# A decoder layer's feed-forward reordered: logits ahead of the shared chunks, an exclusive scan, tiles turned one product sooner

## The chip, the cores and the metric

The kernel runs on one core of a Trainium2 chip. Its time is the device time of one execution in microseconds; the kernel before has a median of 443.64 us in three runs (443.29 to 444.85).

## The reference

A decoder layer for 32 sequences of 128 tokens with 128 features: self attention, attention to a context of 77 tokens, and a feed-forward part with 16 experts, each behind a layer norm and added to x. The change lies in the feed-forward part alone:

```python
logits = hidden @ router_w.T                       # 4096 x 16
top_vals, top_idx = jax.lax.top_k(logits, 1)
scores = sigmoid(top_vals)                         # one expert of 16 per token
gate_up = einsum('nth,nhf->ntf', hidden * scores, gate_up_proj)
routed_out = einsum('ntf,nfh->nth', up * silu(gate), down_proj)
shared = (silu(hidden @ shared_gate_w.T) * (hidden @ shared_up_w.T)) @ shared_down_w.T   # 512 wide
x = x + shared + expert_sum
```

The kernel computes a token's expert only where it is chosen: it sorts the 4096 normalised rows by expert into tiles of 128 rows, each expert's part padded to whole tiles, 47 tiles in all, runs each tile through its expert's weights and scatters the results back.

## The kernel before

**Work.** Tokens are taken in 8 groups of 4 sequences (512 columns). The shared feed-forward of a group is 4 chunks of 128 hidden units, 32 chunks in all. A chunk is: gate product (L1360) and up product (L1361) on TensorE, silu of the gate on ScalarE into `s_g`, product of both on VectorE into `act[c]` (`gated`, L1115), and the down products (L1351) that add up over 4 chunks in one bank, which VectorE adds to `xs` (`add_down`, L1120). A tile n is: load of its rows (`t_row`, issued by ScalarE, L1310) and of its expert's 192 KB of weights (`t_w`, issued by SP, L1444), turn on TensorE (L1397), copy to `t_hT` on ScalarE (L1288), gate and up products (L1406, L1407), silu (L1292), product on VectorE (L1198), down product (L1425), copies of row numbers and result on VectorE (L1204, L1205), and an indirect scatter to `routed` by POOL (L1337).

**Order.** Every engine runs its own written list in order; semaphores join them, no planner is involved. At the end of the attention TensorE turns the normalised rows of a group (`turn_h`), ScalarE copies them to `xT` (`copy_h`), and TensorE makes their logits in bank 1 (`logits`, L1084). With each of the 8 groups one half of a chunk of group 0 goes along (`half_chunk`: even ones gate, odd ones up), so four chunks' gate and up products are made by then. VectorE takes `gated` of chunks 0 to 2, and then, once all logits are there, the maximum (L1129), the one-hot of the first maximum (L1131 to L1135), and the gating score. TensorE counts tokens per expert and ranks them with two products on the one-hot (L1370, L1372), an inclusive scan adds the counts up (L1146), a subtraction makes it exclusive (L1147), six operations on 16 columns make each expert's first tile, three wide ones and a reduction make each token's slot `pos` (L1164). Then `owner`, each tile's expert, follows (L1167 to L1170), on which SP waits. `gated` and `add_down` of groups 0 and 1 stand between these steps. ScalarE scales the normalised rows by their score, four at a time with each of the first 8 chunks from chunk 4 on (L1265); POOL scatters 128 rows at a time, 32 times, to `sorted_in` (L1332).

**Ahead, among and behind the tiles.** The chunks of 6 groups (24) come ahead of the tiles. Of the other 8, three stand among the tiles (behind tiles 14, 28, 42: gate and up in one piece in TensorE's list, down two tiles later), one ahead of the last tile's down product, four behind the tiles. Tile loops are written a tile or two ahead: in turn n, TensorE makes the gate and up products of tile n+1, turns tile n+2 into the single bank 0, and makes tile n's down product; ScalarE copies tile n+2, applies silu to n+1 and issues the row load of tile n+6; VectorE multiplies n+1 and moves n out. There are rings of 8 buffers for rows, weights and results, `t_hT`, `t_sg` and `t_act` have two. ScalarE issues the first 8 row loads once all 32 scatters have landed. SP reads 8 owners into registers, issues 8 weight loads, reads the next 8, and so on; from tile 8 on a load waits for the down product eight tiles back. In the end SP waits for all scatters, loads `routed` back in four pieces, VectorE adds them to `xs` and SP stores 8 groups.

Of the kernel before, what the change touches and what calls it, by code (L numbers as in the profile page):

```python
# [29 lines left out]
def decoder_layer(nc, t, out):  # L30
# [26 lines left out]
    with ExitStack() as ctx:  # L57
# [891 lines left out]
        def act_phase3(a):  # L949
# [38 lines left out]
            deviation3(a, 1)  # L988
# [40 lines left out]
        cum = sb4("cum", [P, N_LG])  # L1029
# [74 lines left out]
        def dve_phase4(v):  # L1104
# [18 lines left out]
            for c in range(CH - 1):  # L1123
                gated(0, c)
# [4 lines left out]
            v.tensor_reduce(best[:], lg3, AX.X, ALU.max).then_inc(s["lg"], 1)  # L1129
            v.wait_ge(s["lg"], 1)  # L1130
# [9 lines left out]
            gated(0, 3)  # L1140
# [4 lines left out]
            cum3 = cum[:].rearrange("p (n b) -> p n b", b=B)  # L1145
            step(v.tensor_tensor_scan(out=cum[:], data0=onesf[:], data1=bank[BK_COUNT][:], initial=0.0, op0=ALU.mult, op1=ALU.add))  # L1146
            step(v.tensor_tensor(tot[:], cum[:], bank[BK_COUNT][:], ALU.subtract))  # L1147
            gated(1, 0)
            first, last = tot3[:, :, 0], cum3[:, :, B - 1]
# [29 lines left out]
            add_down(AHEAD_OF_TILES - 1, (AHEAD_OF_TILES - 1) % 2)  # L1179
# [5 lines left out]
            def behind_add(g):  # L1185
                v.wait_ge(s["downp"], g + 1)
                x_g = seqs(xs, g).rearrange("p j f -> p (j f)")
                v.tensor_tensor(x_g, bank[BEHIND_DOWN[g - AHEAD_OF_TILES]][:], x_g, ALU.add).then_inc(s["x3"], 1)

            def add_routed(g):  # L1190
                if g % 2 == 0:
                    v.wait_ge(y_in[g // 2], 16)
                v.wait_ge(s["x3"], max(g + 1, AHEAD_OF_TILES))
                v.tensor_tensor(xs[:, g * JP:(g + 1) * JP], xs[:, g * JP:(g + 1) * JP], seqs(y_back[g // 2], g % 2), ALU.add).then_inc(s["res_add"], 1)
# [12 lines left out]
            def body(n, r, k):  # L1207
                if not last_tile(n, 1):
                    mul(n + 1, (r + 1) % RING)
                leave(n, r, k)  # L1210
                if n - 1 in MIXED:
                    behind_gated(MIXED[n - 1])
            mul(0, 0)
            loop_tiles(body)
            behind_gated(3)
            behind_gated(4)
            behind_add(6)
            behind_gated(5)
            add_routed(0)
            add_routed(1)  # L1220
            behind_gated(6)
            add_routed(2)
            add_routed(3)
            behind_gated(7)
# [14 lines left out]
        BEHIND_DOWN = (5, 4)  # L1239
        TILE_TURN, TILE_DOWN = 0, (1, 4)  # L1240

        def behind_banks(m):
            return (2, 3) if m in (4, 6) else (6, 7)
# [12 lines left out]
        def act_phase4(a):  # L1256
# [40 lines left out]
            def body(n, r, k):  # L1297
                if not last_tile(n, 2):
                    turned(n + 2, (r + 2) % RING)
                if not last_tile(n, 1):  # L1300
                    gated(n + 1, (r + 1) % RING)
                if n in MIXED:
                    behind_silu(MIXED[n])
                if n >= 2 and not last_tile(n, RING - 2):
                    load_rows(n + (RING - 2), (r + RING - 2) % RING)

            def load_rows(n, r):
                if n >= RING:
                    a.wait_ge(s["ty"], n - (RING - 1))
                a.dma_start(t_row[r][:], sorted_in[bass.ds(n * P, P)]).then_inc(t_in[r], 16)  # L1310
            a.wait_ge(s["scat"], B * 16)
            for r in range(RING):
                load_rows(r, r)
# [4 lines left out]
            for m in range(len(MIXED), BEHIND):  # L1318
                behind_silu(m)

        def pool_phase4(p):
            p.wait_ge(s["bp"], 4 * (NG - 2) * JP)
            p.memset(onesf[:], 1.0)
            p.memset(h_rows[:, :, D:ROW], 0.0).then_inc(s["h_kept"], 1)
# [16 lines left out]
        def pe_phase4(pe):  # L1341
            for g in range(2, NG):
# [3 lines left out]
                half_chunk(pe, g)  # L1346
# [9 lines left out]
            def shared(g, par):  # L1356
                for c in range(CH):
# [9 lines left out]
                    if g == 0 and c == 2:  # L1367

# [3 lines left out]
                        pe.matmul(bank[BK_RANK][:], before[:], oh_b[:], start=True, stop=True).then_inc(s["rankp"], 1)  # L1372
            loop_shared(pe, shared)
            down(AHEAD_OF_TILES - 1, (AHEAD_OF_TILES - 1) % 2, CH - 1)

            def behind_gate_up(m):
                pe.wait_ge(s["act"], BASE + (m if m <= len(MIXED) else m - 1))
                gate, up = behind_banks(m)
                g, c = AHEAD_OF_TILES + m // CH, m % CH
                pe.matmul(bank[gate][:], sg[:, c * P:(c + 1) * P], xT[:, g * GT:(g + 1) * GT], start=True, stop=True)  # L1380
                pe.matmul(bank[up][:], su[:, c * P:(c + 1) * P], xT[:, g * GT:(g + 1) * GT],
                          start=True, stop=True).then_inc(s["gup"], 1)

            def behind_down(m):
                c = m % CH
                pe.wait_ge(s["act"], BASE + m + 1)
                for j in range(JP):
                    i = pe.matmul(bank[BEHIND_DOWN[m // CH]][:, j * D:(j + 1) * D], act[c][:, j * P:(j + 1) * P], sd[:, c],
# [4 lines left out]
            def turn(n, r, k):  # L1393
                pe.wait_ge(t_in[r], k * 32 + 32)
                if n >= 1:
                    pe.wait_ge(s["tT"], n)
                i = pe.transpose(bank[TILE_TURN][:, 0:P], t_row[r][:, 0:D], ident[:])  # L1397
                i.then_inc(s["tTp"], 1)

            def gate_up(n, r):  # L1400
                pe.wait_ge(s["tT"], n + 1)
                if n >= 2:
                    pe.wait_ge(s["tact"], n - 1)
                if n == 1:
                    pe.wait_ge(s["x3"], AHEAD_OF_TILES - 1)
# [3 lines left out]
            def body(n, r, k):  # L1409
                if not last_tile(n, 1):  # L1410
                    gate_up(n + 1, (r + 1) % RING)
                if not last_tile(n, 2):
                    turn(n + 2, (r + 2) % RING, (n + 2) // RING)
                if n in MIXED:
                    behind_gate_up(MIXED[n])
                if n - 2 in MIXED:
                    behind_down(MIXED[n - 2])
                if last_tile(n, 1):
                    behind_gate_up(len(MIXED))
                pe.wait_ge(s["tact"], n + 1)  # L1420
                if n >= 2:
                    pe.wait_ge(s["ty"], n - 1)
                if n == 1:
                    pe.wait_ge(s["x3"], AHEAD_OF_TILES)
# [6 lines left out]
            pe.wait_ge(s["ty"], TILES)  # L1431
            for m in range(len(MIXED) + 1, BEHIND):
                behind_gate_up(m)
# [3 lines left out]
        def sp_phase4(sp):  # L1437
# [8 lines left out]
            load_ring(0, False)  # L1446
            for k in range(1, -(-TILES // RING)):
# [119 lines left out]
```

## Time and profile before

| | |
|---|---|
| median of 3 runs | 443.64 us |
| profiled execution | 446.38 us, span 444.5 us |
| TensorE products, weight loads | 380.0 us (85%), 291.8 us (66%) |
| VectorE, ScalarE, POOL | 282.3 us (63%), 255.3 us (57%), 195.9 us (44%) |
| mean granted TensorE clock | 0.97 |
| moved | 61.83 MB, mean 139 GB/s |

The page cuts the span into 40 slices of 11.1 us and gives in tenths how busy each engine was; the feed-forward part begins at about slice 26. A digit of the DMA row is the mean over the core's 16 transfer engines.

```profile
PE   2789877886768999899899998899999978898894
...
ACT  3688898887446677776777775435532223333311
POOL 1397677555013546555620000000577717676730
PEclk9999999999868999999999999879999999999998
DMA  8962235675827656566610000000061137788629
```

A busy engine need not be the bound: a share is a mean over stages, and what a stage costs is read from the waits in it.

### The profile page before, as it was taken

What the parts mean: (1) busy time and instruction counts of PE and PEld (TensorE: products, weight loads), DVE (VectorE), ACT (ScalarE), POOL (GpSimd) and SP (SyncE); (2) the same over time, 40 slices, a digit from 0 to 9 for tenths busy, and PEclk for the clock granted to TensorE, in tenths of its full rate; (3) what the DMA queues carried; (4) which work ended last, traced back from release to release, by engine and by line L of the source; (5) the groups of instructions that cost most, each with busy time, mean ns of one, the idle gap of its engine ahead of it and who ended that gap; (6) DMA issues with size and microseconds to landing.
All of it is one profiled execution on the core that took longest, in us unless ns stands there. A gap on an engine that the chain in (4) does not pass through costs nothing.

```text
span 444.5 us, 10412 instructions
## 1 busy us (share of the span) xinstructions
PE 380.0 (85%) x3691; PEld 291.8 (66%) x3691; DVE 282.3 (63%) x837; ACT 255.3 (57%) x611; POOL 195.9 (44%) x280
## 2 busy tenths in 40 slices
PE   2789877886768999899899998899999978898894
PEld 1466655664546888888888887675566656677663
DVE  4566999989477777877877736527633324444436
ACT  3688898887446677776777775435532223333311
POOL 1397677555013546555620000000577717676730
PEclk9999999999868999999999999879999999999998
DMA  8962235675827656566610000000061137788629
GB/s 268 350 192 67 97 97 149 182 189 160 253 73 216 155 165 186 159 177 191 193 45 6 5 4 2 1 1 0 32 196 56 49 94 230 225 251 236 202 81 327
DMA packets 45050, 61.83 MB, mean 139 GB/s; under 512 B 7308, under 2 KB 40972, under 8 KB 43388
## 3 DMA queue, kind: packets, MB, share of 16 engines
q1 hardware_dynamic: 33400, 37.63, 28.0%
q0 software_dynamic: 4832, 20.37, 15.7%
q10 hardware_dynamic: 6768, 3.18, 2.9%
q8 instruction: 30, 0.49, 0.5%
q14 instruction: 20, 0.16, 0.1%
HBM read 43.34 MB, written 20.59 MB: 144 GB/s over the span
## 4 chain that ended last, share of the span: by engine, by line
PE 59%; DVE 19%; ACT 9%; issue 6%; DMA 4%; ACTq 1%; POOL 0%; DVEq 0%; SPq 0%; POOLq 0%
PE bank L801 7%; PE bank L790 6%; PE bank L1351 4%; PE bank L762 4%; PE bank L1360 3%; PE bank L1361 3%; PE bank L1406 3%; DVE res_q L359 3%; ACT xn L427 3%; PE bank L825 2%; PE bank L615 2%; DVE mx L868 2%; DMA t_row<-sorted_in 2%; ACT t_hT L1288 2%; PE bank L600 2%
## 5 line engine op out<-in xcount | busy, mean ns | idle before, releaser
L954 ACT ACTIVATE prob<-bank 77x512 f32<-77x512 f32 x128 | 74.5, 596 | 19.0 <-PE bank L790 18.9
L1332 POOL DMA_INDIRECT sorted_in<-h_rows,pos_s x32 | 31.5, 985 | 85.6 <-ACT h_rows L1265 77.0
L868 DVE TENSOR_REDUCE mx<-bank 128x5 f32<-128x385 f32 (+1 forms) x96 | 54.7, 575 | 22.2 <-PE bank L762 19.6
L1337 POOL DMA_INDIRECT routed<-t_y,t_no x47 | 45.4, 966 | 27.5 <-DVE t_y L1205 17.7
L790 PE MATMUL bank<-qst,kst 99*77 99x128 bf16 x512 | 50.8, 223 | 0.5 <-ACT prob L954 0.3
L1261 ACT ACTIVATE s_g<-bank 128x512 f32<-128x512 f32 x32 | 19.1, 598 | 47.3 <-PE bank L1361 33.7
L790 PEld LDWEIGHTS bank<-qst,kst 99*77 99x77 bf16 x512 | 39.1, 117 | 7.8 <-ACT prob L954 4.0
L1115 DVE TENSOR_TENSOR act<-bank,s_g 128x512 f32<-128x512 f32 x24 | 16.5, 688 | 39.9 <-ACT s_g L1261 39.9
L762 PE MATMUL bank<-kst,qst 96*128 96x77 bf16 x512 | 34.5, 203 | 6.7 <-DVE mx L868 6.6
L1288 ACT COPY t_hT<-bank 128x128 f32<-128x128 f32 x47 | 12.5, 266 | 39.1 <-PE bank L1397 34.1
L801 PE MATMUL bank<-prob,vals 77*17 77x128 f32 x1024 | 34.6, 274 | 0.0
L1351 PEld LDWEIGHTS bank<-sd,act 128*128 128x128 f32 x192 | 24.8, 192 | 13.1 <-issue 9.9
L1198 DVE TENSOR_TENSOR t_act<-bank,t_sg 128x128 f32<-128x128 f32 x47 | 13.7, 292 | 30.4 <-ACT t_sg L1292 30.3
L762 PEld LDWEIGHTS bank<-kst,qst 96*128 96x128 bf16 x512 | 26.8, 100 | 9.6 <-DVE mx L868 7.4
L427 ACT ACTIVATE xn<-xs,ln_bias,ln_rstd 128x128 f32<-128x128 f32 x64 | 26.5, 494 | 9.7 <-DVE ln_bias L339 9.7
L541 POOL TENSOR_TENSOR qkv<-qkv,rn 128x256 f32<-128x256 f32 x32 | 19.1, 629 | 26.4 <-ACT rn L480 26.4
L721 POOL DMA_DIRECT2D qst<-qparts x30 | 15.0, 498 | 34.6 <-DMA kst<-kparts 32.7
L1406 PE MATMUL bank<-t_hT,t_w 128*128 128x128 f32 x94 | 22.3, 319 | 7.2 <-ACT t_hT L1288 2.1
L801 PEld LDWEIGHTS bank<-prob,vals 77*17 77x17 f32 x1024 | 25.3, 97 | 3.0 <-issue 0.2
L1351 PE MATMUL bank<-sd,act 128*128 128x128 f32 x192 | 25.5, 276 | 1.4 <-DVE act L1115 1.3
L615 PE MATMUL bank<-first_pack,xnT 128*128 128x384 f32 x64 | 24.8, 535 | 1.9 <-ACT xnT L470 1.9
L961 ACT COPY avs_s<-bank 128x512 f32<-128x512 f32 x32 | 18.8, 586 | 13.2 <-PE bank L801 13.2
(165 smaller groups left out, 942.1 us busy)
## 6 DMA issues: line engine op xcount, KB each, us to landing
qst<-qparts POOLq DMA_DIRECT2D x36, 256.0 KB, 3.5
t_w<-in_expert_w SPq DMA_DIRECT2D x47, 192.0 KB
qparts<-qpart SPq DMA_DIRECT2D x16, 384.0 KB, 4.9
kst<-kparts POOLq DMA_DIRECT2D x36, 154.0 KB, 3.9
kparts<-kpart SPq DMA_DIRECT2D x16, 231.0 KB, 3.7
sorted_in<-in_fill SPq DMA_DIRECT2D x1, 3102.0 KB, 14.3
t_row<-sorted_in ACTq DMA_DIRECT2D x47, 66.0 KB
qst<-qparts SPq DMA_DIRECT2D x12, 256.0 KB, 4.6
```

The source lines that it names most:

```text
L427: i = a.activation(dst[:, j], x_of(g, j), ACT.Identity, scale=ln_rstd[k][:, j:j + 1], bias=ln_bias[k][:, j:j + 1])
L615: pe.matmul(bank[1 + j][:, 0:3 * D], xnT[g % 2][:, j * P:(j + 1) * P], wqkv[:], start=True, stop=True).then_inc(s["qkvp"], 1)
L762: i = pe.matmul(bank[n % 2][:, (h - h0) * KEYS:(h - h0 + 1) * KEYS], qst[r][0:ROWS, h, c * S:(c + 1) * S], kst[r][0:ROWS, h, c * KEYS:(c + ...
L790: i = pe.matmul(bank[2 + n % 2][0:KEYS, c * S:(c + 1) * S], kst[r][0:SHIFT_ROWS, h, t * KEYS:(t + 1) * KEYS], qst[r][0:SHIFT_ROWS, h, t * ...
L801: i = pe.matmul(bank[AV_BANK[b % 2]][32 * c:32 * c + EX + 1, u * P:(u + 1) * P], vals[:, b, 4 * u + c], prob[n % PROBS][:, c], start=True, ...
L868: v.tensor_reduce(mx[:, b % JA, h0:h1], bank[n % 2][:, 0:(h1 - h0) * KEYS].rearrange("p (h k) -> p h k", k=KEYS), AX.X, ALU.max, negate=Tr ...
L954: a.activation(prob[n % PROBS][:].rearrange("p c t -> p (c t)"), bank[2 + n % 2][0:KEYS], ACT.Exp, scale=SCORE_SCALE).then_inc(s["expd"], 1)
L1288: a.copy(t_hT[r % 2][:], bank[TILE_TURN][:, 0:P]).then_inc(s["tT"], 1)
L1332: p.indirect_dma_start(out=sorted_in, out_offset=bass.IndirectOffsetOnAxis(ap=pos[:, b:b + 1].bitcast(U32), axis=0), in_=h_rows[:, b], in_ ...
L1337: p.indirect_dma_start(out=routed, out_offset=bass.IndirectOffsetOnAxis(ap=t_no[r][:].bitcast(U32), axis=0), in_=t_y[r][:], in_offset=None ...
L1351: i = pe.matmul(bank[BK_DOWN[par]][:, j * D:(j + 1) * D], act[c][:, j * P:(j + 1) * P], sd[:, c], start=(c == 0 and j == 0), stop=(c == CH ...
L1406: pe.matmul(bank[2 + r % 2][:, 0:P], t_w[r][:, 0:FF], t_hT[r % 2][:], start=True, stop=True)
```

## The change

Six edits, all in the feed-forward part:

1. ScalarE copies group 3 ahead of the last `deviation3` instead of behind it, and leaves silus 1 to 3 of group 0 until the copies are done; TensorE leaves the half chunks 4 to 7 behind the logits (4 and 5 right behind, 6 and 7 behind counts and ranks, which come one chunk sooner in the loop).
2. VectorE's list puts the maximum behind `gated(0, 0)`, and the other chunk products one by one between the ranking's steps.
3. `cum` is one column longer with a zero in column 0, which makes the scan exclusive by a view; the subtraction goes.
4. Five groups come ahead of the tiles instead of six. Of the 12 chunks left, three come ahead of the tile loop, five among the tiles (behind tiles 4, 12, 20, 28, 36: gate at that tile, up one tile later, down four tiles later), one ahead of the last down, three behind the tiles. One bank (5) takes all their down products, with adds by VectorE at tiles 9 and 41.
5. In the tile loop TensorE turns tile n+2 ahead of the gate and up products of tile n+1 instead of behind them.
6. SP instead of ScalarE issues the first 8 row loads, between its first and second ring of weight loads.

```diff
 # act_phase4
             for g in range(3, NG):
                 copy_h(a, g)
-                if g % 2 == 1:
-                    c = (g - 3) // 2
-                    silu(c, BK_GATE[c % 2], c + 1)
+                if g == 3:
+                    deviation3(a, 1)
+                    silu(0, BK_GATE[0], 1)
+            silu(1, BK_GATE[1], 2)
             a.wait_ge(s["lg"], 1)
             a.activation(score[:], best[:], ACT.Exp, scale=-1.0).then_inc(s["escore"], 1)
-            silu(CH - 1, BK_GATE[(CH - 1) % 2], CH)
+            for c in range(2, CH):
+                silu(c, BK_GATE[c % 2], c + 1)
...
 # dve_phase4
-            for c in range(CH - 1):
-                gated(0, c)
+            gated(0, 0)
             v.wait_ge(s["lgp"], NG)
...
             v.tensor_reduce(best[:], lg3, AX.X, ALU.max).then_inc(s["lg"], 1)
+            gated(0, 1)
             v.wait_ge(s["lg"], 1)
...
-            gated(0, 3)
+            gated(0, 2)
...
-            step(v.tensor_tensor_scan(out=cum[:], ...))
-            step(v.tensor_tensor(tot[:], cum[:], bank[BK_COUNT][:], ALU.subtract))
-            gated(1, 0)
+            step(v.tensor_tensor_scan(out=cum[:, 1:N_LG + 1], ...))
...
             step(v.scalar_tensor_tensor(out=adj[:], in0=adj[:], scalar=float(P), in1=first, ...))
-            gated(1, 1)
-            add_down(0, 0)
-            step(v.tensor_tensor(tot3, tot3, bc(adj[:], B), ALU.add))
+            gated(0, 3)
+            step(v.tensor_tensor(tot3, below3, bc(adj[:], B), ALU.add))
...
             step(v.tensor_tensor(wrk[:], wrk[:], oh_b[:], ALU.mult))
+            gated(1, 0)
             step(v.tensor_reduce(low[:], wrk3, AX.X, ALU.add))
             v.tensor_copy(pos[:], low[:]).then_inc(s["pos"], 1)
+            gated(1, 1)
+            add_down(0, 0)
             gated(1, 2)
...
-        AHEAD_OF_TILES = 6
+        AHEAD_OF_TILES = 5
-        MIXED = {14: 0, 28: 1, 42: 2}
+        FIRST_MIXED = 3
+        MIXED = {4: 3, 12: 4, 20: 5, 28: 6, 36: 7}
+        DOWN_AFTER = 4
+        DOWN_DONE = {8: 0, 40: 1}
...
 # pe_phase4
-                half_chunk(pe, g)
+                if g < 4:
+                    half_chunk(pe, g)
+            half_chunk(pe, 4)
+            half_chunk(pe, 5)
...
-                    if g == 0 and c == 2:
+                    if g == 0 and c == 1:
                         pe.wait_ge(s["oh"], 1)
...
+                        half_chunk(pe, 6)
+                        half_chunk(pe, 7)
...
             def body(n, r, k):
+                if not last_tile(n, 2):
+                    turn(n + 2, (r + 2) % RING, (n + 2) // RING)
                 if not last_tile(n, 1):
                     gate_up(n + 1, (r + 1) % RING)
-                if not last_tile(n, 2):
-                    turn(n + 2, (r + 2) % RING, (n + 2) // RING)
                 if n in MIXED:
-                    behind_gate_up(MIXED[n])
-                if n - 2 in MIXED:
-                    behind_down(MIXED[n - 2])
+                    behind_gate(MIXED[n])
+                if n - 1 in MIXED:
+                    behind_up(MIXED[n - 1])
+                if n - DOWN_AFTER in MIXED:
+                    behind_down(MIXED[n - DOWN_AFTER])
...
+            behind_gate(0)
+            behind_up(0)
+            down(AHEAD_OF_TILES - 1, (AHEAD_OF_TILES - 1) % 2, CH - 1)
+            behind_gate(1)
+            behind_up(1)
+            behind_down(0)
+            behind_gate(2)
+            behind_up(2)
             turn(0, 0, 0)
+            behind_down(1)
+            turn(1, 1, 0)
             gate_up(0, 0)
-            turn(1, 1, 0)
+            behind_down(2)
             loop_tiles(body)
...
 # sp_phase4
             load_ring(0, False)
+            sp.wait_ge(s["scat"], B * 16)
+            for r in range(RING):
+                sp.dma_start(t_row[r][:], sorted_in[bass.ds(r * P, P)]).then_inc(t_in[r], 16)
             for k in range(1, -(-TILES // RING)):
                 load_ring(k * RING, True)
```

## Rows read from the trace of the kernel before

**Rows 1.** Chain of waits from 300 us on, a chunk's pieces: start us, us, what.
```profile
352.89 0.86 PE bank L1361 x2
...
353.75 0.89 PE bank L1351 x8
```
**Rows 2.** Window table, router's stretch: us, busy (and count) by engine, PEclk, DMA share, GB/s.
```profile
core 0: us, PE busy (x) PEld busy (x) DVE busy (x) ACT busy (x) POOL busy (x), PEclk, DMA share, GB/s
290.00:295.00 5.00, 5.00 (x20) 3.86 (x18) 0.00 (x0) 0.59 (x1) 0.00 (x0) 0.50 0.00 0
```
**Rows 3.** Timeline, 285 to 298 us: start, us, engine, line, operation, count [idle before].
```profile
285.19 0.58 ACT L1079 COPY xT<-bank 128x512 f32<-128x512 f32 x1
...
289.73 1.06 PE L1074 MATMUL bank<-first_pack,h_rows 128*128 128x128 f32 x4
...
290.58 1.73 PE L1084 MATMUL bank<-rw,xT 128*128 128x16 f32 x8
...
292.15 2.05 PE L1094 MATMUL bank<-xT,su 128*128 128x512 f32 x2
...
293.99 1.06 PE L1074 MATMUL bank<-first_pack,h_rows 128*128 128x128 f32 x4
...
297.85 0.69 DVE L1129 TENSOR_REDUCE best<-bank 128x32 f32<-128x512 f32 x1 [0.95 <-PE bank L1084]
```
**Rows 4.** Timeline, VectorE's ranking, 300 to 314 us.
```profile
300.75 0.69 DVE L1135 TENSOR_TENSOR oh_b<-wrk,low 128x512 bf16<-128x512 f32 x1
...
302.83 1.22 DVE L1146 TENSOR_TENSOR_SCAN cum<-onesf,bank 128x512 f32<-128x512 f32 x1 [0.36 <-PE bank L1372]
...
307.81 0.19 DVE L1156 SCALAR_TENSOR_TENSOR adj<-adj,tot 128x16 f32<-128x16 f32 x1
...
309.95 0.68 DVE L1159 TENSOR_TENSOR tot<-tot,adj 128x512 f32<-128x512 f32 x1
...
313.21 0.18 DVE L1164 CAST pos_s<-low 128x32 int32<-128x32 f32 x1
```
**Rows 5.** Timeline of POOL: first and last of 32 sorting scatters.
```profile
314.23 1.54 POOL L1332 DMA_INDIRECT sorted_in<-h_rows,pos_s  x1 [76.13 <-ACT h_rows L1265]
...
354.22 0.97 POOL L1332 DMA_INDIRECT sorted_in<-h_rows,pos_s  x1 [0.31 <-issue]
```
**Rows 6.** Timeline, from the sorted rows to the first routed scatter.
```profile
356.74 3.72 ACTq L1310 DMA_DIRECT2D t_row<-sorted_in  x8
...
358.77 0.27 PE L1397 MATMUL bank<-first_pack,t_row 128*128 128x128 f32 x1
...
364.15 0.97 POOL L1337 DMA_INDIRECT routed<-t_y,t_no  x1 [8.97 <-DVE t_y L1205]
```
**Rows 7.** Timeline, one unmixed tile, 362 to 364 us.
```profile
362.32 0.39 PE L1407 MATMUL bank<-t_hT,t_w 128*128 128x128 f32 x2
...
362.85 0.27 ACT L1288 COPY t_hT<-bank 128x128 f32<-128x128 f32 x1 [0.73 <-PE bank L1397]
...
363.33 0.29 DVE L1198 TENSOR_TENSOR t_act<-bank,t_sg 128x128 f32<-128x128 f32 x1 [0.88 <-ACT t_sg L1292]
...
364.03 0.27 ACT L1288 COPY t_hT<-bank 128x128 f32<-128x128 f32 x1 [0.73 <-PE bank L1397]
```
**Rows 8.** Timeline of POOL: routed scatter behind a mixed chunk, and the last of 47.
```profile
386.05 0.97 POOL L1337 DMA_INDIRECT routed<-t_y,t_no  x1 [1.42 <-DVE t_y L1205]
...
427.14 0.97 POOL L1337 DMA_INDIRECT routed<-t_y,t_no  x1 [0.37 <-DVE t_y L1205]
```
**Rows 9.** SP's weight loads by timeline, chain of waits, and waits ahead of t_row's readers.
```profile
371.44 0.33 SPq L1444 DMA_DIRECT2D t_w<-in_expert_w  x1
...
376.52 0.33 SPq L1444 DMA_DIRECT2D t_w<-in_expert_w  x1
...
369.92 4.80 DMA t_row<-sorted_in
...
  DMA t_row<-sorted_in: 1.0, 3
```
**Rows 10.** Window table, the last stretch.
```profile
432.00:444.50 12.50, 6.80 (x36) 4.50 (x35) 7.57 (x12) 1.36 (x3) 0.00 (x0) 0.91 0.97 328
```

More of the change, by code:

```diff
@@ L1144, in dve_phase4 @@
             tot3 = tot[:].rearrange("p (n b) -> p n b", b=B)
-            cum3 = cum[:].rearrange("p (n b) -> p n b", b=B)
-            step(v.tensor_tensor_scan(out=cum[:], data0=onesf[:], data1=bank[BK_COUNT][:], initial=0.0, op0=ALU.mult, op1=ALU.add))
-            step(v.tensor_tensor(tot[:], cum[:], bank[BK_COUNT][:], ALU.subtract))
-            gated(1, 0)
-            first, last = tot3[:, :, 0], cum3[:, :, B - 1]
+            below3 = cum[:, 0:N_LG].rearrange("p (n b) -> p n b", b=B)
+            upto3 = cum[:, 1:N_LG + 1].rearrange("p (n b) -> p n b", b=B)
+            step(v.tensor_tensor_scan(out=cum[:, 1:N_LG + 1], data0=onesf[:], data1=bank[BK_COUNT][:], initial=0.0, op0=ALU.mult, op1=ALU.add))
+            first, last = below3[:, :, 0], upto3[:, :, B - 1]
             step(v.scalar_tensor_tensor(out=cnt_i[:], in0=last, scalar=float(P - 1), in1=first, op0=ALU.add, op1=ALU.subtract))
@@ L1187, in behind_add @@
                 x_g = seqs(xs, g).rearrange("p j f -> p (j f)")
-                v.tensor_tensor(x_g, bank[BEHIND_DOWN[g - AHEAD_OF_TILES]][:], x_g, ALU.add).then_inc(s["x3"], 1)
+                v.tensor_tensor(x_g, bank[BEHIND_DOWN][:], x_g, ALU.add).then_inc(s["x3"], 1)
             def add_routed(g):
@@ L1307, in load_rows @@
             def load_rows(n, r):
-                if n >= RING:
-                    a.wait_ge(s["ty"], n - (RING - 1))
+                a.wait_ge(s["ty"], n - (RING - 1))
                 a.dma_start(t_row[r][:], sorted_in[bass.ds(n * P, P)]).then_inc(t_in[r], 16)
-            a.wait_ge(s["scat"], B * 16)
-            for r in range(RING):
-                load_rows(r, r)
+            for m in range(FIRST_MIXED):
+                behind_silu(m)
             turned(0, 0)
@@ L1317, in act_phase4 @@
             loop_tiles(body)
-            for m in range(len(MIXED), BEHIND):
+            for m in range(MIXED_END, BEHIND):
                 behind_silu(m)
@@ L1323, in pool_phase4 @@
             p.memset(onesf[:], 1.0)
+            p.memset(cum[:, 0:1], 0.0)
             p.memset(h_rows[:, :, D:ROW], 0.0).then_inc(s["h_kept"], 1)
@@ L1372, in shared, with behind_gate, behind_up @@
                         pe.matmul(bank[BK_RANK][:], before[:], oh_b[:], start=True, stop=True).then_inc(s["rankp"], 1)
+                        half_chunk(pe, 6)
+                        half_chunk(pe, 7)
             loop_shared(pe, shared)
[L1374 to L1378, printed above, removed]
+            def behind_gate(m):
+                pe.wait_ge(s["act"], BASE + (m - 1 if m < FIRST_MIXED or m > MIXED_END else m))
+                if m == 2:
+                    pe.wait_ge(s["x3"], AHEAD_OF_TILES - 1)
                 g, c = AHEAD_OF_TILES + m // CH, m % CH
-                pe.matmul(bank[gate][:], sg[:, c * P:(c + 1) * P], xT[:, g * GT:(g + 1) * GT], start=True, stop=True)
-                pe.matmul(bank[up][:], su[:, c * P:(c + 1) * P], xT[:, g * GT:(g + 1) * GT],
+                pe.matmul(bank[behind_banks(m)[0]][:], sg[:, c * P:(c + 1) * P], xT[:, g * GT:(g + 1) * GT], start=True, stop=True)
+            def behind_up(m):
+                g, c = AHEAD_OF_TILES + m // CH, m % CH
+                pe.matmul(bank[behind_banks(m)[1]][:], su[:, c * P:(c + 1) * P], xT[:, g * GT:(g + 1) * GT],
                           start=True, stop=True).then_inc(s["gup"], 1)
@@ L1396, in turn @@
                     pe.wait_ge(s["tT"], n)
+                if n == 0:
+                    pe.wait_ge(s["silu"], BASE + 1)
                 i = pe.transpose(bank[TILE_TURN][:, 0:P], t_row[r][:, 0:D], ident[:])
```

60 lines of the change are left out of this document (36 added, 24 removed).

## The prediction

> **What bounds the kernel now.** I read the chain of waits from 300 us on first, then the window table, then the timelines of the stretches that the chain names. The diff touches four sections of it. Up to 302 us the router decides: logits one after another on TensorE, then VectorE ranks them. From 302 to 357 us the chain is TensorE's shared chunks, 0.86 + 0.86 + 0.89 = 2.61 us each [rows 1]. Beside them POOL sends the 32 sorting scatters, from 314.23 to 354.22, 0.97 us each and 0.30 between, a floor of 1.27 [rows 5], and ScalarE's first row load, which waits for the last of them to land, goes at 356.74, just as TensorE ends its last chunk [rows 6]. Two paths of one length end there: only a change that shortens both moves the tiles. From 364.15 to 427.14 POOL scatters 47 tiles, a mean of 62.99 / 46 = 1.369 us; its floor is again 1.27, and what is over it are gaps such as the 1.42 behind a mixed chunk [rows 6, 8]. Last come the loads back, adds and stores, with the transfer engines 0.97 busy at 328 GB/s in the last 12.5 us [rows 10].
>
> **Logits earlier.** The clock granted from 290 to 295 us is 0.50, the level of 1.2 GHz [rows 2]. In it a turn of four takes 0.85 us (289.73 to 290.58), four logits 1.57 (290.58 to 292.15), a half chunk 1.84 (292.15 to 293.99) [rows 3]. Three half chunks leave the way of the last logits. The copy of group 3 (0.6) no longer stands between the deviation and the table load, so group 4's copy goes at 284.7 where it went at 285.19 and ends at 285.3; its logits start at 285.4. From there four logits and two turns come before the last logits' own end: groups 4 to 7 and the turns of 6 and 7, 4 x 1.57 + 2 x 0.85 = 8.0. The maximum starts at 293.45 where it started at 297.85 [rows 3]: -4.4 us. If the higher clock returned sooner, up to 2 more.
>
> **Ranking.** The chunk product gated(0,1) now stands between the maximum and the steps to the one-hot: +0.65, nearly its own length of 0.7. From the one-hot's end (301.44) to the scan (302.83) stays 1.39, and gated(0,2) fits into it. From the scan to the end of the positions passed 313.39 - 302.83 = 10.56 [rows 4]. Now: scan 1.25; six small steps of 0.2 each, 1.3 (the last begins at 307.81); gated(0,3) 0.7; the wide steps from 309.95 to 313.39, 3.44, with gated(1,0) among them, 0.8: 7.5. What is gone is the subtraction, a wait for ScalarE's silu ahead of gated(1,0), gated(1,1) and the add behind it. -3.05. Sum: -4.4 + 0.65 - 3.05 = -6.8. Positions at 306.6, POOL's first scatter at 307.4, its last landed at 356.74 - 6.8 = 349.9. POOL is kept fed: ScalarE scales four rows with each chunk of 2.61 us and POOL needs 5.1 us for four.
>
> **Chunks ahead of the tiles.** TensorE's own path: one-hot at 301.44 - 4.4 + 0.65 = 297.7, counts and ranks 1.1 (the time up to 302.6), two half chunks 1.72 and two downs 1.78: 302.3. Sixteen chunks of 2.61 = 41.8: 344.1. Then gate and up of three chunks (5.16) and two downs (1.78): 351.0. I add 0.4 for waits on VectorE's ranking: TensorE is at the first turn at 351.4.
>
> **First rows by SP.** SP has nothing else then. The first load landed at most 358.77 - 356.74 = 2.03 us after its issue [rows 6], so the first turn is at 349.9 + 2.1 = 352.0 and the rows decide by 0.6. From there to the first routed scatter 364.15 - 358.77 = 5.38 us passed, with ScalarE issuing all eight loads (3.72 us) ahead of the first copy. After the change the copy goes at once, but two downs of shared chunks (1.8) stand between: I work out 4.6 by the pieces (turn and copy 0.6, down 1.0, product 0.7, down 0.9, turn and next product 0.8, down and leaving 0.6). SP pays: its register loads for tiles 8 to 15 come behind the row issues. Eight issues of 0.5 = 4.1, then 376.52 - 371.44 = 5.1 from one ring's last issue to the next ring's first [rows 9]: tile 8's weights go at 359.1 instead of being ready to go at once. If they take 3 us they land at 362, a tile later than its turn (352.0 + 2.7 + 6 x 1.0 = 361), which POOL's lead of two tiles covers; with 4.8, the longest landing on the chain, 2 us are lost once. First routed scatter 352.0 + 4.6 = 356.6; I take 357.05 for small stalls: -7.1 (bounds -5.6, with both stalls, and -8.0).
>
> **A turn sooner.** Now a tile is a ring of copy, product, turn, copy: 362.85 to 364.03, 1.18 us [rows 7]. With the turn ahead of the product, the copy hides under it. What is left is TensorE's work: three products of 128 columns at a quarter of the chunk's 0.86 [rows 1], 0.22 each, and a turn at an eighth of the 0.85 that four take at half clock [rows 3], 0.11, together 0.77; and the ring of product, silu, multiplication and down: the product ends at 362.71, the multiplication at 363.62, a down could start at 363.68, 0.98 later [rows 7]. That ring spans two tiles: (0.98 + 0.39 for a down that has waited, as the 0.39 of 362.32, + 0.55 for turn and product) / 2 = 0.96 us a tile. 46 x 0.96 + five chunks of 2.61 + 1.72 for the gate and up ahead of the last down = 58.9; POOL's floor is 46 x 1.272 = 58.5. (The same sum for before, 46 x 1.18 + 3 x 2.61 + 1.72, gives 63.8 against 62.99 measured.) TensorE and POOL are nearly equal, so each sometimes waits: I add 0.9 to the floor, 59.4, which is -3.6 us. Bounds: 58.5, and 63.0 with no gain if the tile stays at 1.05. Cutting the mixed chunk into three pieces is counted at nothing: the products are the same and fill TensorE's waits; without that cover they cost their 2.61, which the 58.9 holds in full.
>
> **The tail.** One chunk fewer behind the tiles frees TensorE of 2.6 and VectorE of 0.7 us. But the transfers fill the last 12.5 us at 0.97 [rows 10], so an earlier add only queues. I take -0.1 (bounds -0.7 and +0.5).
>
> **Sum.** -7.1 - 3.6 - 0.1 = -10.8. The profiled execution took 446.38 us (span 444.5), so 435.6; the median of the runs, 443.64, lies 2.74 below it, so 432.8 us. The forecast's own range, from the bounds with tiles -1.5 to -4.5: 430.4 to 437.0. Chance 0.56.
>
> **Rivals.**
> 1. The row loads set the tiles' rate. A row load is issued four turns ahead of its own. Now the issue falls with the copy, 0.3 us after a turn; it comes to stand behind the gated silu, 0.95 after. Four tiles take at least landing time plus 0.95. Only three of 47 loads held TensorE up [rows 9], at a slack of 4 x 1.18 - 0.3 = 4.4; one of them took 4.80. At 4.8 the tile takes (4.8 + 0.95) / 4 = 1.44. If half the tiles do and half take 1.29: 62.8, -0.2 in place of -3.6, 436.2 us; if all, 66.2, 439.6. Against it: nearly all loads landed within 4.4, and POOL's rate leaves 4 x 1.27 - 0.95 = 4.1. Chance 0.22.
> 2. The clock stays low without the half chunks, and TensorE, not the rows, decides the start. If 0.50 lasts through counts and ranks, two half chunks 3.7 and a down 1.8 reach 298.9 instead of 297.7 and counts and ranks take 1 us more: positions at 308.8, and TensorE gets to the first turn at 354 to 355. Start -4.5 in place of -7.1: 435.4. For it: the low stretch began among just such turns. Against: it also ended among them. Chance 0.12.
> 3. Slower than before: the ring of rival 1 with landing times over any seen, because SP sends six weight loads in a row after its register loads while four tiles now run closer together. To give back the 7.2 of start and tail a tile must take (63.0 + 7.2) / 46 = 1.53, a landing of 5.15 us. At 5.5: 1.61, 74.2 us, 443.64 - 7.2 + 11.2 = 447.6. Chance 0.05.
> 4. It does little of what it says: the ranking still waits for silus, TensorE waits for the ranking, and the mixed chunks open the same gaps at POOL (five instead of three): start -2, tiles +0.5, 442. Chance 0.05.
>
> The Trainium skill, page "TensorE: Matmul & The Clock Gate", section "Part 4: PE-mode transpose", says that transposes done by TensorE do not count as busy for its clock as products do. By that a stretch with fewer half chunks would hold 1.2 GHz longer: rival 2, and -8.2 in place of -10.8. The trace bears it out only in part: the low clock was granted with half chunks among the turns too.
>
> **Chances.** A difference under 0.5% (2.2 us) is about what a measurement cannot tell from no change. Faster: 0.56 + 0.12 + 0.20 of rival 1, less 0.01: 0.87. Same: 0.02 of rival 1, 0.04 of rival 4, 0.01: 0.07. Slower: 0.05 of rival 3, 0.01: 0.06. Range 429.8 to 438.5: the low side takes in a clock that returns early and a POOL without gaps, the high side most of rival 1.
>
> **What would show it.** The maximum near 293.5, positions near 306.6; POOL's first sorting scatter near 307.4, its first routed one near 357, its last near 416.5, most of them 1.27 apart; the first turn waiting for a row load; TensorE's products no longer waiting for ScalarE's copy. A clock of 0.50 past 297 us is rival 2, turns that wait for row loads in many tiles are 1 or 3, gaps over 1 us at each mixed chunk are 4.

## The result and the profile after

The changed kernel takes 432.52 us (median of 4 runs, 431.79 to 433.76) where the kernel before took 444.25 in the same runs: a ratio of 0.9751, 95% interval 0.9702 to 0.9800, so 11 us faster. The prediction was 432.8 us. The profiled execution took 431.88 us, span 430.0: 14.5 us shorter than the profiled one before, some 3.4 us more than the timed ratio gives. Most of that surplus is TensorE's clock, below.

The timeline of the changed kernel, same columns as [rows 3 to 8]:

```profile
289.40 0.69 DVE L1127 TENSOR_REDUCE best<-bank 128x32 f32<-128x512 f32 x1 [4.42 <-PE bank L1083]
...
302.17 0.18 DVE L1162 CAST pos_s<-low 128x32 int32<-128x32 f32 x1
...
303.19 1.06 POOL L1344 DMA_INDIRECT sorted_in<-h_rows,pos_s  x1 [65.54 <-DVE pos_s L1162]
...
343.10 0.97 POOL L1344 DMA_INDIRECT sorted_in<-h_rows,pos_s  x1 [0.30 <-issue]
...
345.42 3.65 SPq L1487 DMA_DIRECT2D t_row<-sorted_in  x8
...
347.32 0.33 PE L1420 MATMUL bank<-first_pack,t_row 128*128 128x128 f32 x1 [0.22 <-DMA t_row<-sorted_in]
...
351.72 0.96 POOL L1349 DMA_INDIRECT routed<-t_y,t_no  x1 [7.64 <-DVE t_y L1204]
...
413.23 0.97 POOL L1349 DMA_INDIRECT routed<-t_y,t_no  x1 [0.30 <-issue]
```

Read in pairs, each row gives a section. To set executions side by side I measure from ScalarE's last deviation (`std<-mv,eps` over 4 columns), which starts at 282.38 us before and at 281.82 after; what lies ahead of it was not touched.

| section, us | before | after | change | foretold |
|---|---|---|---|---|
| deviation to maximum | 15.47 | 7.58 | -7.89 | -4.4 |
| maximum to positions | 15.36 | 12.77 | -2.59 | -2.4 |
| positions to first turn | 45.56 | 45.15 | -0.41 | 0 |
| first turn to first routed scatter | 5.38 | 4.40 | -0.98 | -0.8, and +0.45 for stalls |
| 47 routed scatters | 62.99 | 61.51 | -1.48 | -3.6 |
| last scatter to end | 17.36 | 16.77 | -0.59 | -0.1 |

The first turn waits 0.22 us for a row load, so both paths still end within a quarter of a microsecond of each other. In the tiles POOL still has gaps. TensorE's waits from 350 us on (releaser: us in total, times, longest), and one of them in the timeline:

```profile
PE bank L1420 <- DMA t_w<-in_expert_w: 3.4, 4, 1.9
PE bank L1420 <- DMA t_row<-sorted_in: 0.9, 2, 0.6
```

```profile
370.00 0.33 SPq L1482 DMA_DIRECT2D t_w<-in_expert_w  x1
...
375.24 0.85 SPq L1482 DMA_DIRECT2D t_w<-in_expert_w  x2
...
379.77 0.33 PE L1420 MATMUL bank<-first_pack,t_row 128*128 128x128 f32 x1 [1.89 <-DMA t_w<-in_expert_w]
...
381.73 0.97 POOL L1349 DMA_INDIRECT routed<-t_y,t_no  x1 [1.80 <-DVE t_y L1204]
```

SP issues the last weights of one ring at 370.00, reads eight owners into registers, issues tile 24's weights at 375.24; the turn of tile 24 waits 1.89 us for them, and POOL has its longest gap, 1.80. In the chain of waits from 350 to 420 us SP's register reads (L1478) stand for 14.5% and the weights' transfers for 16.7%.

Not every gap of POOL is TensorE's. At scatter 24 (the first is 0) nine of the ten profiles off the slower chip have a gap of 0.66 to 1.57 us, 1.24 in the changed kernel, and in all nine the scatter starts 1.33 us after the end of the copy that the profile names as its releaser, where 0.28 is enough elsewhere. In turn_late, a run below:

```profile
387.64 0.28 DVE L1204 COPY t_y<-bank 128x128 f32<-128x128 f32 x1
389.26 0.96 POOL L1349 DMA_INDIRECT routed<-t_y,t_no  x1 [1.57 <-DVE t_y L1204]
```

What it is stays open. The tenth, owners_early, shows no gap there: TensorE was so far ahead of POOL that the copy had ended 1.39 us before.

The clock is in the window table (last three columns: granted clock, transfer share, GB/s). The changed kernel:

```profile
285.00:290.00 5.00, 5.00 (x41) 4.61 (x41) 0.60 (x1) 3.13 (x5) 0.00 (x0) 0.93 0.00 0
290.00:295.00 5.00, 5.00 (x15) 2.42 (x14) 4.42 (x10) 2.15 (x4) 0.00 (x0) 0.73 0.01 2
```

Before, 0.50 was granted for about 10 us and all last logits fell into it [rows 2, 3]; here it is 3.4 us in sum and begins at 289, when the logits are done.

### The profile page after: what moved, and what is told of

The parts are those of the page before. It is cut to its first block, busy times and chain, and to the rows that moved or that the text cites. A ratio compares the mean times of both kernels' runs of the same rounds, so it can differ in the third digit from the quotient of the medians.

```text
span 430.0 us, 10417 instructions
## 1 busy us (share of the span) xinstructions
PE 368.5 (86%) x3691; PEld 288.0 (67%) x3691; DVE 280.1 (65%) x836; ACT 260.0 (60%) x611; POOL 196.4 (46%) x281
## 4 chain that ended last, share of the span: by engine, by line
PE 44%; DVE 17%; DMA 10%; issue 8%; ACT 7%; SPq 7%; POOL 5%; POOLq 0%; DVEq 0%; ACTq 0%
PE bank L801 8%; PE bank L790 6%; POOL sorted_in L1344 5%; PE bank L762 4%; DMA ctxT<-in_ctxT 3%; ACT xn L427 3%; DVE res_q L359 3%; DMA t_w<-in_expert_w 3%; DVE mx L868 3%; PE bank L825 3%; SPq L1478 3%; DMA t_row<-sorted_in 2%; PE bank L1366 2%; PE bank L810 2%; DVE rn L365 2%
## 5 line engine op out<-in xcount | busy, mean ns | idle before, releaser
L1349 POOL DMA_INDIRECT routed<-t_y,t_no x47 | 45.6, 970 | 24.6 <-DVE t_y L1204 14.5
L801 PE MATMUL bank<-prob,vals 77*17 77x128 f32 x1024 | 35.7, 282 | 0.0
L1114 DVE TENSOR_TENSOR act<-bank,s_g 128x512 f32<-128x512 f32 x20 | 13.8, 688 | 24.1 <-ACT s_g L1272 24.1
L1366 PEld LDWEIGHTS bank<-sd,act 128*128 128x128 f32 x160 | 21.0, 193 | 9.6 <-issue 9.6
L615 PE MATMUL bank<-first_pack,xnT 128*128 128x384 f32 x64 | 23.7, 516 | 1.9 <-ACT xnT L470 1.9
L992 POOL TENSOR_TENSOR xs<-xs,second_pack 128x128 f32<-128x128 f32 x32 | 14.9, 474 | 17.7 <-ACT xn L427 17.3
L825 PE MATMUL bank<-fcw,avnT 128*128 128x128 f32 x128 | 22.2, 296 | 0.8 <-ACT avnT L967 0.5
```

Of the source, the lines that this page charges most:

```text
L615: pe.matmul(bank[1 + j][:, 0:3 * D], xnT[g % 2][:, j * P:(j + 1) * P], wqkv[:], start=True, stop=True).then_inc(s["qkvp"], 1)
L801: i = pe.matmul(bank[AV_BANK[b % 2]][32 * c:32 * c + EX + 1, u * P:(u + 1) * P], vals[:, b, 4 * u + c], prob[n % PROBS][:, c], start=True, ...
L825: i = pe.matmul(bank[7][:, FC], avnT[:, k * P:(k + 1) * P], fcw[:, k], start=(k == 0), stop=(k == 1))
L1349: p.indirect_dma_start(out=routed, out_offset=bass.IndirectOffsetOnAxis(ap=t_no[r][:].bitcast(U32), axis=0), in_=t_y[r][:], in_offset=None ...
L1366: i = pe.matmul(bank[BK_DOWN[par]][:, j * D:(j + 1) * D], act[c][:, j * P:(j + 1) * P], sd[:, c], start=(c == 0 and j == 0), stop=(c == CH ...
```

## The experiments

All ratios are to the kernel before, timed beside each run on the same chip in five rounds. Three chips were used. front_only, front_old, turn_late and owners_early ran on one (the kernel before: 445.95 us), the three runs whose names end in _b and late_one_piece on another of the same speed (443.48). changed_again, late_owners, rows_act and owners_one_piece ran on a third, the slower chip, on which every kernel, the one before too (490.46 us), took some 10% longer; their ratios are compared with each other only. Readings by section come from one profiled execution each, and executions of one kernel differ by some microseconds: differences of that size need the ratios behind them.

**front_only.** Before, with the router part alone: half chunks behind the logits, VectorE's new order, the exclusive scan.

```diff
-                half_chunk(pe, g)
+                if g < 4:
+                    half_chunk(pe, g)
+            half_chunk(pe, 4)
+            half_chunk(pe, 5)
...
```

> The kernel before with only the new router order (logits ahead of the half chunks, VectorE's new ranking order, exclusive scan); 24 chunks still come ahead of the tiles, ScalarE still issues the first rows, turns as before. Theory A, two paths of one length: POOL's first sorting scatter comes 11 us earlier (near 303), but TensorE still has four chunks more (10.4 us) than the changed kernel, so the tiles start only as far earlier as TensorE gets through its own list, about 5 us: 439 us. Theory B, POOL's scatters alone hold the tiles: the whole 11 us come through, 433 us.

443.29 us, ratio 0.998 (0.9945 to 1.0015): nothing that can be told from no change. Its last sorting scatter starts at 345.01 where it was 354.22 [rows 5], and yet:

```profile
351.71 3.72 ACTq L1312 DMA_DIRECT2D t_row<-sorted_in  x8
...
354.07 0.27 PE L1404 MATMUL bank<-first_pack,t_row 128*128 128x128 f32 x1
```

The row loads go 6.70 us behind the last scatter (2.3 to 2.5 elsewhere): ScalarE was still in the silus of TensorE's chunks. 4.8 us of the deviation-to-first-scatter stretch are won (81.77 to 76.94), of which some 1.7 is clock (0.50 for 6.8 instead of 10.2 us), and 0.7 is lost at the end. Theory A was right in kind (the start is held by TensorE's and ScalarE's own lists), and its 439 us too hopeful.

**front_old.** The changed kernel with the router part of before.

```diff
             for g in range(2, NG):
                 if g + 1 < NG:
                     turn_h(pe, g + 1)
                 logits(pe, g)
-                if g < 4:
-                    half_chunk(pe, g)
-            half_chunk(pe, 4)
-            half_chunk(pe, 5)
+                half_chunk(pe, g)
...
```

> The changed kernel with the router order of before (half chunks among the logits, old ranking order, inclusive scan and subtraction). Theory A, two paths: TensorE reaches the first turn early and waits for the last sorting scatter, which lands at about 356.5, so the first turn is near 358.5 and the first routed scatter near 363: 11 us over the changed kernel, 443.5 us. Theory B, the shorter list of chunks carries the gain: 437 us. If the lower clock is what the old order causes, the window from 285 to 295 us shows 0.50 for about 10 us again, against 3.3 us in the changed kernel.

445.09 us, ratio 0.9961 (0.9910 to 1.0012). TensorE is early and waits:

```profile
351.95 3.65 SPq L1480 DMA_DIRECT2D t_row<-sorted_in  x8
...
353.94 0.48 PE L1413 MATMUL bank<-first_pack,t_row 128*128 128x128 f32 x1 [4.77 <-DMA t_row<-sorted_in]
```

So the router part alone is worth 0.2%, everything else alone 0.4% (neither clear of no change), both together 2.5%. Maximum to positions takes 15.35 us again, as before. The expectation on the clock failed: in this execution of the old order 1.2 GHz was not granted in the router's stretch,

```profile
285.00:290.00 5.00, 5.00 (x30) 3.50 (x29) 1.38 (x2) 2.67 (x5) 0.00 (x0) 1.00 0.00 0
290.00:295.00 5.00, 5.00 (x34) 3.94 (x33) 2.33 (x4) 3.34 (x5) 0.00 (x0) 1.00 0.00 0
```

and its maximum comes 10.68 us after the deviation, where [rows 3] gave 15.47. The same instructions, with the same 1.20 us idle ahead of them, hold the clock in one execution and not in the other.

The low clock came later instead, and it is part of what this run pays. TensorE had been idle for the 4.77 us of its wait, and 0.50 was granted from 351.9 to 358.7 us:

```profile
352.00:358.00 6.00, 4.06 (x19) 4.06 (x20) 0.29 (x1) 0.81 (x3) 0.00 (x0) 0.50 0.40 90
```

The eight down products behind the first turn take 1.92 us here and 1.06 in the changed kernel, and the first routed scatter comes 6.63 us after the first turn (360.57), not 4.40. The profiled execution took 439.80 us, 5.3 under this run's median; the 4.8 us that it saved in the router's stretch are about that difference (an estimate: the others were not profiled).

**turn_late.** The changed kernel with turn and products in the old order.

```diff
-                if not last_tile(n, 2):
-                    turn(n + 2, (r + 2) % RING, (n + 2) // RING)
                 if not last_tile(n, 1):
                     gate_up(n + 1, (r + 1) % RING)
+                if not last_tile(n, 2):
+                    turn(n + 2, (r + 2) % RING, (n + 2) // RING)
```

> The changed kernel with the turn of tile n+2 behind the products of tile n+1 again. Theory A, the ring of copy, product, turn sets a tile's pace: 1.18 us a tile, 46 x 1.18 + 5 x 2.61 + 1.72 = 69 us from POOL's first to last routed scatter where the changed kernel takes 61.5: 440 us. Theory B, weights that SP issues late set the pace, whatever the order on TensorE: 0 to 2 us, 432.5 to 434.5.

435.92 us, ratio 0.9819 (0.9769 to 0.9868). 47 scatters in 61.72 us (355.77 to 417.49), 0.2 over the changed kernel, not 7.5. Theory A's sum was wrong. Theory B was right on the tiles (0 to 2 us) for another reason than it gave, since here no turn waits for weights, and the median lies 1.4 us over its range. The turns show why so little is lost:

```profile
383.79 0.27 PE L1420 MATMUL bank<-first_pack,t_row 128*128 128x128 f32 x1
...
384.97 0.27 PE L1420 MATMUL bank<-first_pack,t_row 128*128 128x128 f32 x1
...
386.14 0.27 PE L1420 MATMUL bank<-first_pack,t_row 128*128 128x128 f32 x1
...
387.82 0.27 PE L1420 MATMUL bank<-first_pack,t_row 128*128 128x128 f32 x1
```

A plain tile takes its 1.18 us, which is under POOL's 1.27, and a tile with a piece of a chunk 1.64 to 1.68: the three pieces cost some 1.4 us a chunk and not the 2.61 of theory A. TensorE needs 58.84 us from turn 2 to turn 46; POOL's floor for these 44 steps is 44 x 1.27 = 55.9, and the 2.9 between them are about what the scatters take over their own floor (61.72 for 58.5). The rest of its profile's 4 us is ahead of the tiles (the deviation 2.35 us later, a maximum in the low clock). By the ratios (0.9819, and 0.9751 for the changed kernel) the late turn costs 0.7 points, 3 us, with intervals that overlap; the profiles show only 0.2 of it in the tiles.

**late_one_piece.** turn_late, and gate and up of a mixed chunk together.

```diff
-                if n in MIXED:
-                    behind_gate(MIXED[n])
                 if n - 1 in MIXED:
+                    behind_gate(MIXED[n - 1])
                     behind_up(MIXED[n - 1])
```

> The changed kernel with the turn behind the products and the gate and up products of a mixed chunk in one stretch: the tile loop as before but for where its chunks stand and that there are five. The run turn_late took 61.7 us where the ring of 1.18 us with five whole chunks gives 69. Theory A, the pieces fill the ring's waits: in one stretch each chunk costs about 1 us again, 65 to 67 us, ratio near 0.99. Theory B, POOL's rate hides chunks and ring alike, pieces or not: 62 us as turn_late.

436.22 us, ratio 0.9833 (0.9774 to 0.9892), 63.70 us of scatters, 2.0 over turn_late: between the theories. At four of the five chunks POOL's gap is larger by 0.4 to 0.8. The ratios of the two runs (0.9819 for turn_late) don't tell them apart. Here late_one_piece, then turn_late, at the same chunk:

```profile
362.02 0.97 POOL L1349 DMA_INDIRECT routed<-t_y,t_no  x1 [1.08 <-DVE t_y L1204]
```

```profile
362.52 0.96 POOL L1349 DMA_INDIRECT routed<-t_y,t_no  x1 [0.67 <-DVE t_y L1204]
```

**owners_early.** The changed kernel with SP's owner reads spread.

```diff
-                expert = [sp.value_load(owner[0:1, bass.ds(n0 + r, 1)], ...) for r in here]
...
+            def load_weights(n):
+                r = n % RING
+                if n >= RING:
+                    sp.wait_ge(s["tyd"], n + 1 - RING)
+                sp.dma_start(t_w[r][:], t["expert_w"][bass.ds(expert[r], 1)]...)
+                if n + RING < TILES:
+                    expert[r] = owner_of(n + RING)
```

> The changed kernel, but SP reads the owner of tile n+8 right behind the weight load of tile n, instead of eight owners in one go at the head of each ring of eight. Theory A, these eight register reads (5.1 us between the last load of a ring and the first of the next) make TensorE wait for weights at a ring's head: its 3.4 us of waits for t_w and POOL's gaps at tiles 24 and 26 go, POOL's 47 scatters take 58.6 to 59.5 us instead of 61.5: 430 us. Theory B, the transfer engines are full and the weights land late anyway: within 0.5 us of the changed kernel, 432.

430.43 us, ratio 0.9714 (0.9665 to 0.9763). Scatters from 351.73 to 410.20: 58.47 us, POOL's floor, with no gap. The edit also moves the reads for tiles 8 to 15 ahead of the first row loads, so tile 8's weights are issued at 350.96 and not at 354.06. TensorE's waits for weights are gone, and so are SP's reads from the chain of waits; what TensorE still waits for:

```profile
PE bank L1409 <- DVE act L1182: 3.9, 1, 3.9
PE bank L1420 <- DMA t_row<-sorted_in: 1.3, 3, 0.5
```

(The 3.9 stands behind the tiles.) **owners_early_b**, the same kernel again:

> owners_early again, as the measure beside the others of this call: 58.5 us for the 47 scatters, all 1.27 apart, and no wait of a turn for weights over 0.5 us. A first result of 61.5 would say that the gain seen before was chance.

430.21 us, ratio 0.9699 (0.9645 to 0.9753), but in this profile the scatters took 61.80 us:

```profile
PE bank L1420 <- DMA t_row<-sorted_in: 2.9, 3, 2.3
```

A row load held TensorE 2.3 us once, and the tiles that TensorE was ahead of POOL were used up (gaps of 1.32 and 1.58). So with the weights out of the way rival 1 is what is left, now and then. The expectation had said that 61.5 us would make the first profile's gain chance. The 61.80 us meet that sign, though not by weights: no turn waits for them in either profile. This profiled execution took 435.63 us, 5.4 over the median of its run. The two ratios agree; against the changed kernel's 0.9751 and 0.9747 they are lower by 0.4 to 0.5 points (2 us), with intervals that overlap. That the reads cause the waits for weights is shown; that spreading them gains time is likely and not clear of noise.

**late_owners_b.** owners_early with the late turn. (A first run, **late_owners**, on the slow chip: 0.9729, 0.9683 to 0.9775, beside 0.9747 for the changed kernel; its tiles can't be read, for the reason told at the end.)

> Turn behind the products as before, and SP's owner reads spread as in the run owners_early. Theory A, two limits of about one size hid each other: with the reads spread the ring of copy, product, turn shows, and the 47 scatters take about 61.7 us as in turn_late, 3 us over owners_early: 433.5 us. Theory B, the turn's place costs nothing once chunk pieces fill its waits: 58.5 us, as owners_early, 430.5.

> late_owners once more, since in its first profile ScalarE stood still for tens of microseconds ahead of the tiles in all kernels. Theory A, the late turn's ring and SP's owner reads were two limits of one size: 61.7 us for the 47 scatters, 3 us over owners_early. Theory B, the turn's place is worth nothing with the chunk in three pieces: 58.5 to 59 us.

434.28 us, ratio 0.9773 (0.9713 to 0.9833), scatters in 61.89 us. Eight gaps of 0.47 to 1.57, and no turn waits for a transfer. The profiled execution took 437.25 us, 3.0 over the median. It is theory A by the first profile of owners_early (58.47, so 3.4 us), and no difference by the second (61.80). The medians on this chip, 434.28 and 430.21, say 4 us, with intervals of the ratio that overlap; on the slower chip late turn and spread reads (0.9729) are no slower than the changed kernel (0.9747), and owners_early was not run there. The gaps are those of turn_late, within 0.02 us at seven of the eight tiles, so with the late turn the reads make no difference that shows.

**owners_one_piece_b** (first run **owners_one_piece** on the slow chip: 0.9773, 0.9723 to 0.9824). owners_early with gate and up together.

> owners_early with gate and up products of a mixed chunk in one stretch of 1.72 us on TensorE instead of two of 0.86 a tile apart. Theory A, POOL's lead covers a stretch of this size: 58.5 us from first to last routed scatter, 430.4 us. Theory B, the pieces are what keeps POOL fed: a gap of 0.5 to 0.9 us at each of the five chunks, 61 to 63 us, 433 to 434.5.

> owners_one_piece again on an undisturbed start. Theory A, with the early turn TensorE is so far ahead that POOL's lead covers a stretch of 1.72 us: 58.5 us as owners_early. Theory B, pieces are needed in any case: gaps at the five chunks, 60 to 62 us.

431.93 us, ratio 0.9749 (0.9695 to 0.9804), scatters in 59.73 us, gaps of 0.80 and 1.04 and TensorE waiting for rows 2.3 us in all. 1.3 over the first profile of owners_early and under the second; the ratios (0.9749 and 0.9699) overlap: not settled.

**rows_act** (slow chip). ScalarE issues the first eight row loads.

```diff
-            sp.wait_ge(s["scat"], B * 16)
+            a.wait_ge(s["scat"], B * 16)
             for r in range(RING):
-                sp.dma_start(t_row[r][:], sorted_in[bass.ds(r * P, P)]).then_inc(t_in[r], 16)
+                a.dma_start(t_row[r][:], sorted_in[bass.ds(r * P, P)]).then_inc(t_in[r], 16)
```

> The changed kernel with the first eight row loads issued by ScalarE again. Theory A: its 3.7 us of issuing stand ahead of the first copies, first turn to first routed scatter goes from 4.4 back to about 6 us, and POOL, which sets the tiles' rate, never wins that back: +1.5, 434 us. Theory B: SP's owner reads for tiles 8 to 15 come 9 us earlier, TensorE's 0.65 us wait for tile 8's weights goes and POOL's gaps shrink by as much as the start lost: 432.5.

Ratio 0.9852 (0.9793 to 0.9912) beside 0.9747 (0.9699 to 0.9795) for **changed_again**, the changed kernel beside it.

> The changed kernel itself, as the measure for the three runs beside it and for how far TensorE's granted clock moves from one execution to the next. Its router stretch may hold 0.50 for anything from 0 to 10 us (0.0 us and 10.2 us were seen with the same old order); the tiles' 47 scatters should take 61.5 us again, since register reads and turns don't depend on it.

In rows_act the first turn is at 383.67, and the copy behind it stands behind the issues:

```profile
385.62 0.27 ACT L1301 COPY t_hT<-bank 128x128 f32<-128x128 f32 x1 [3.17 <-issue]
...
390.74 0.97 POOL L1352 DMA_INDIRECT routed<-t_y,t_no  x1 [43.52 <-DVE t_y L1204]
```

7.07 us from turn to scatter against 4.53 in changed_again: 2.5 us, in part again low clock (0.50 from 385.5 to 388.9, behind a TensorE that had waited 1.85 us for the rows and 1.15 for the copy). It is theory A, and more than the 1.5 it gave. The 1.05 points of ratio are 5.1 us on this chip; the 2.6 beyond the first scatter are not explained, and the intervals just overlap.

## Why the prediction was right

That 432.8 came within 0.3 us of the measured 432.52 is in part luck: some terms were too large and others too small. What follows takes them in order.

**Two paths of one length** held, and is the main lesson: front_only and front_old shorten one path each and gain 0.2% and 0.4%, neither clear of no change, together 2.5%.

**Ranking** was worked out right: -2.4 foretold, -2.59 measured, 15.35 again with the order undone. (In the eight profiles of the new order off the slower chip the stretch takes 12.7 to 12.8 us five times and 13.4 to 13.7 three times; the reason stands with rival 2 below.)

**Logits earlier** came out at -7.89 for -4.4, for a reason that was no part of the step. Without low clock the old order takes 10.68 us (front_old) and the new 7.58: -3.1 is the order's own. The other 4.8 of the profile is a clock stretch that the execution before had and front_old had not. The step carried rows of one execution over as if the clock belonged to the code. The new order isn't free of it either: it had 0.50 for 3.4 to 6.8 us in its eight profiles off the slower chip, where the old one had it for 0 and 10.2. In the changed kernel's profile and in owners_early's it began with the wide products of the half chunks, after the logits. In the other six it began before the maximum, which then came 8.1 to 9.4 us after the deviation. Rival 2 did not come in the changed kernel: the low clock ended at 292.7 us, ahead of the counts at 293.6, and the rows, not TensorE, decided the first turn. A small piece of it came in front_only, late_one_piece and owners_one_piece_b, where TensorE, slowed by the low clock, makes the counts 4.9 to 5.1 us after the maximum instead of 4.1 to 4.3. Whether fewer half chunks hold the low clock longer, as the rule of the Trainium skill on transposes (page "TensorE: Matmul & The Clock Gate", section "Part 4: PE-mode transpose") would have it, is left open. Two executions of the old order and eight of the new don't give its frequency.

**That clock also accounts for the surplus of the profiles.** 10.2 us at half clock before against 3.4 after are (10.2 - 3.4) / 2 = 3.4 us of TensorE's work, and 4.8 on the way to the maximum, as all of the 10.2 lay ahead of it and the 3.4 behind. 14.5 less 3.4 to 4.8 is 9.7 to 11.1; the ratio gives 444.25 x 0.0249 = 11.1.

**First rows by SP.** The rows decided, by 0.22 us where 0.6 was foretold, and 4.40 us to the first scatter where 4.6 was worked out. The price on SP was looked for at tile 8, and there TensorE waits 0.65 us. But every later ring has the same 5.2 us of register reads at its head (370.00 to 375.24 above). They stood in the kernel before too, 5.1 us [rows 9], and no turn waited for weights there; with turns that come sooner they no longer fit. Together it is the 3.4 us of waits for weights.

**A turn sooner** is the step that failed in its size: -3.6 was foretold for the tiles and -1.48 came. Rival 1 in its first form (row loads) has 0.9 us of TensorE's waits, weights have 3.4. With the reads spread the same tiles reached 58.47 us in one profile of two, as good as the step's floor of 58.5. TensorE went from turn 2 to turn 46 in 53.07 us there, and in 58.84 with the late turn: its sum for TensorE was about right. The gain lay behind limits that it had not priced: the weights above all, and at scatter 24 the gap that is not TensorE's. And by the profiles what did come is hardly the turn's: the runs with the late turn split -1.48 into +0.7 for two more chunks (63.70), -2.0 for the pieces (61.72) and -0.2 for the turn. The two profiles with late turn and pieces agree (61.72 and 61.89), those of the early turn spread from 58.47 to 61.80, and the ratios would give the turn some 3 us, so the split's last term is not settled. "Counted at nothing" was wrong for the pieces. With a late turn a chunk costs TensorE 1.8 us over its plain tiles in one stretch and 1.4 in pieces (60.82 and 58.84 us from turn 2 to turn 46), and POOL's scatters follow, 63.70 and 61.72. In the kernel before it cost 2.6 (two tiles of 2.5).

**The tail** gave 0.6, not 0.1. VectorE is done early and waits for the loads back:

```profile
419.81 1.29 DVE L1193 TENSOR_TENSOR xs<-xs,y_back 128x512 f32<-128x512 f32 x2 [3.43 <-DMA y_back<-routed]
```

Eight profiles off the slower chip with three chunks behind the tiles end 16.5 to 17.1 us after the last scatter, the two with four chunks 17.4 and 18.1.

So the total was right with terms that were off both ways. Ahead of the tiles -7.1 was foretold, and -11.9 in the profile, less 3.4 to 4.8 of clock, is -7.1 to -8.5. In it the logits' own -3.1 fall short of -4.4, and the smaller sections make up for it. The tiles gave -1.5 for -3.6, the tail -0.6 for -0.1. That adds up to -9.2 to -10.6 where -10.8 was foretold and the ratio gives -11.1; the clock of the timed executions, which one profile can't give, is what is left.

## What to carry to other kernels

Where two engines' lists end at one wait, trace both to it before pricing an edit: shortening one alone may be worth nothing. Where a loop is made faster, price every fixed block that recurs in it, such as a ring's register reads, and not only its first occurrence. Take the granted clock out of a single profile before carrying its durations over.

## What the hardware showed beyond that

On the slower chip both kernels lose some 46 us. In the changed kernel's profiles 31 of them lie between positions and first turn (76.46 us for 45.15) and 12 in the tiles (73.92 for 61.51), where POOL scatters. In changed_again ScalarE stands still twice, for nothing that the trace names ("remote"), while SP's eight weight loads stretch from 4.03 us to 18.26:

```profile
323.26 18.26 SPq L1482 DMA_DIRECT2D t_w<-in_expert_w  x8
331.77 0.60 ACT L1272 ACTIVATE s_g<-bank 128x512 f32<-128x512 f32 x1 [12.34 <-remote]
...
352.81 1.09 ACT L1272 ACTIVATE s_g<-bank 128x512 f32<-128x512 f32 x2 [19.29 <-remote]
```

POOL's sorting scatters kept their 1.27 us meanwhile. The ratio, 0.9747, was the same there. What stalls the engines stays open; it was not tried.
